# Attention logits of a graph network: four buffers of lifted one-hots, running maxima over five chunk slots, maxima between the small logit steps

## The reference, cut to what matters

```python
h = x @ Wn.T + bn
e = edge_attr @ We.T + be
xj = h[src]
a = leaky_relu(sum((xj + e) * attn, axis=-1), 0.01)     # one logit per edge
m = segment_max(a, dst, num_segments=N)                 # greatest logit of each destination node
a = exp(a - m[dst])
a = a / (segment_sum(a, dst, num_segments=N)[dst] + 1e-16)
out = relu(segment_sum(xj * a[:, None], dst, num_segments=N))
```

## Time and profile before

| | us |
|---|---|
| median of three runs | 4340.02 (4337.76 to 4342.67) |
| the profiled execution, its own time | 4305.89 |
| its span, first to last instruction | 4304.1 |
| stretch of the logit steps, first `expand` of the block loop to the end of the last reduction | 426.7 |

### The profile page before, as it was taken

How to read it: one execution, slowest core, us unless ns; L and a number is a source line. 1 busy time by engine, 2 the same in 40 slices (tenths; PEclk the granted TensorE clock), 3 DMA queues, 4 the chain that set the end, 5 groups by cost and what they waited for, 6 DMA issues and landing times. The chain is left out here.

```text
span 4304.1 us, 87013 instructions
## 1 busy us (share of the span) xinstructions
PE 3335.9 (78%) x18482; PEld 2452.3 (57%) x18483; DVE 2751.1 (64%) x9374; ACT 1717.5 (40%) x5555; POOL 1143.8 (27%) x908
## 2 busy tenths in 40 slices
PE   5555556888888885999943335899998699998988
PEld 4333335777777774676732224777887344544455
DVE  7999999999898884325478886777665300000453
ACT  1555552234344552102178875777774100000111
POOL 1788888888888000101000000000000000000002
PEclk9999999999999997999955557999999899999998
DMA  2444442556677774666666553433331253543046
GB/s 101 116 109 114 111 111 71 141 166 210 197 214 237 275 282 158 182 198 186 196 189 189 181 166 114 152 122 121 106 108 40 93 194 119 182 154 84 3 173 252
DMA packets 437987, 658.37 MB, mean 153 GB/s; under 512 B 98732, under 2 KB 294167, under 8 KB 437762
## 3 DMA queue, kind: packets, MB, share of 16 engines
q1 hardware_dynamic: 354306, 526.63, 38.9%
q10 hardware_dynamic: 53040, 121.95, 7.8%
q0 software_dynamic: 30544, 8.56, 2.8%
HBM read 440.04 MB, written 216.02 MB: 152 GB/s over the span
## 5 line engine op out<-in xcount | busy, mean ns | idle before, releaser
L1007 POOL DMA_INDIRECT slots<-all_B,put_index x800 | 1051.6, 1315 | 342.9 <-issue 237.8
L1889 POOL MEMSET c_T<- 128x28 f32 x1 | 0.1, 148 | 1983.3 <-POOLq L138 1983.3
L770 DVE TENSOR_SCALAR put_hot<-all_iota_bf,put_words_in 128x125 bf16<-128x125 bf16 x2400 | 443.7, 318 | 3.3 <-DMA put_words_in<-slots 3.3
L2437 DVE TENSOR_TENSOR upd_pre<-upd_po,upd_bias 125x512 f32<-125x512 f32 x25 | 17.3, 692 | 621.5 <-PE upd_po L2368 621.5
L1253 ACT ACTIVATE lm_raised<-lm_hot,srt_words 128x125 f32<-128x125 bf16 x1200 | 356.3, 385 | 83.4 <-DVE lm_top L1168 67.8
L981 PE MATMUL put_ps<-put_right_in,put_left_in 128*128 128x125 f32 x2380 | 340.3, 293 | 51.1 <-ACT put_left_in L840 49.1
L1288 PE MATMUL lm_ps<-lm_v,lm_node 125*128 x1220 | 170.2, 184 | 267.2 <-DVEq L1155 95.4
L2012 PE MATMUL att_ps<-att_right,att_left 128*125 128x125 f32 x2380 | 319.5, 286 | 67.2 <-ACT att_right L2033 63.9
L981 PEld LDWEIGHTS put_ps<-put_right_in,put_left_in 128*128 128x128 f32 x2380 | 300.2, 201 | 76.2 <-ACT put_left_in L840 57.9
L2012 PEld LDWEIGHTS att_ps<-att_right,att_left 128*125 128x125 f32 x2380 | 287.0, 190 | 95.7 <-issue 82.2
L840 ACT CAST put_left_in<-put_hot 128x640 f32 (+1 forms) x238 | 173.8, 730 | 415.0 <-DVE put_hot L770 398.3
(11 more groups left out here) (393 smaller groups left out, 5797.6 us busy)
## 6 DMA issues: line engine op xcount, KB each, us to landing
c_T<-counts SPq DMA_DIRECT2D x255, 312.5 KB, 3.3
pair<-put_T ACTq DMA_DIRECT2D x125, 625.0 KB
hot<-put_hot SPq DMA_DIRECT2D x480, 160.0 KB
att_ring<-hot SPq DMA_DIRECT2D x240, 320.0 KB
gio_T<-pair SPq DMA_DIRECT2D x60, 1250.0 KB, 5.9
all_A<-in_edge_attr_dram SPq DMA_DIRECT2D x100, 448.0 KB
lm_planes<-src_rows SPq DMA_DIRECT2D x123, 320.0 KB, 3.7
counts<-put_T ACTq DMA_DIRECT2D x125, 312.5 KB
```

Of the source, the lines that this page charges most:

```text
L770: ins = v.tensor_scalar(hot[:, h, t, c * S:c * S + P], k["iota_bf"][:, :], words_in[:, j, c, t:t + 1], None, ALU.is_equal)
L1007: nc.gpsimd.indirect_dma_start(slots, bass.IndirectOffsetOnAxis(index[:, C * g + j:C * g + j + 1], 0), stage[:, C * g + j, :], None).then_ ...
```

## The change

`raised` gets four buffers (`RING`) in place of two, each split in two halves `u` of five chunks. The running maximum `top` has five chunk slots (625 numbers) in place of ten, and there are two of it, used in turn by even and odd blocks. The first group of a block takes the maximum of its two halves; every other group takes two maxima of 625 numbers, one for each half. In the step, the first maximum stands between the sum and the addition of the edge part, the second between the leaky relu and the subtraction of the floor. The wait for `lifted` moves ahead of the addition. A new semaphore `halved` orders the two maxima. The wait for `joined` at the top of a block now asks for the reduction of the block before the last one.

```diff
-        raised, top8, tops = s.sb("raised", [L, 2, G * P]), s.sb("top8", [L, G * P]), negated
+        raised, top, tops = s.sb("raised", [L, RING, 2, HALF * P]), s.sb("top", [L, 2, HALF * P]), negated
...
-                def total(chain, g):
+                def totals(chain, g):
                     dve.wait_ge(looked, g + 3)
                     chain(v.tensor_reduce(z[:, :], ps[:, ds((g % PZ) * 512, 3 * G)].rearrange("p (c t) -> p c t", t=3), AX.X, ALU.add))
                     dve.sem_inc(summed, 1)
+
+                def with_edges(chain, g):
                     chain(v.tensor_tensor(z[:, :], z[:, :], logit[:, ds(G * g, G)], ALU.add))
...
-                def greater(g, first):
-                    lift = raised[:, ds(g % 2, 1), :].rearrange("p a n -> p (a n)")
-                    dve.wait_ge(lifted, g + 4)
-                    dve.wait_ge(grouped, g + 2)
-                    if first:
-                        ins = v.tensor_copy(top8[:, :], lift)
-                    else:
-                        ins = v.tensor_tensor(top8[:, :], top8[:, :], lift, ALU.max)
-                    ins.then_inc(grouped, 1)
+                def lift(g, u):
+                    return raised[:, ds(g % RING, 1), u, :].rearrange("p a n -> p (a n)")
...
-                for sem, head in ((summed, PZ), (grouped, 2), (joined, 1), (expanded, 2)):
+                for sem, head in ((summed, PZ), (grouped, RING), (joined, 1), (expanded, 2)):
...
-                def step(g, first):
+                def step(d, g, first):
                     chain = Chain(dve, chain_sem, n + 3 * g)
+                    of_block = top[:, ds(d % 2, 1), :].rearrange("p a n -> p (a n)")
                     expand(g + 3)
                     dve.wait_ge(ready, g + 2)
-                    total(chain, g + 2)
-                    logits(chain, g + 2)
-                    greater(g, first)
+                    totals(chain, g + 2)
+                    dve.wait_ge(lifted, g + 4)
+                    if not first:
+                        dve.wait_ge(grouped, g + RING)
+                        v.tensor_tensor(of_block, of_block, lift(g, 0), ALU.max).then_inc(halved, 1)
+                    with_edges(chain, g + 2)
+                    if first:
+                        v.tensor_tensor(of_block, lift(g, 0), lift(g, 1), ALU.max).then_inc(grouped, 1)
+                        dve.sem_inc(halved, 1)
+                        logits(chain, g + 2)
+                    else:
+                        chain(v.scalar_tensor_tensor(z[:, :], z[:, :], 0.01, z[:, :], ALU.mult, ALU.max))
+                        dve.wait_ge(halved, g + 1)
+                        v.tensor_tensor(of_block, of_block, lift(g, 1), ALU.max).then_inc(grouped, 1)
+                        v.tensor_scalar(logit[:, ds(G * (g + 2), G)], z[:, :], floor[:, :], None, ALU.subtract).then_inc(ready, 1)
...
-                    dve.wait_ge(joined, d + 1)
+                    dve.wait_ge(joined, d)
                     dve.sem_inc(passed, 1)
-                    step(g0, True)
+                    step(d, g0, True)
                     with dve.Fori(g0 + 1, g1) as g:
-                        step(g, False)
-                    dve.wait_ge(grouped, g1 + 2)
+                        step(d, g, False)
+                    dve.wait_ge(grouped, g1 + RING)
                     v.tensor_reduce(tops[:, ds(d, 1), :].rearrange("p a n -> p (a n)"),
-                                    top8[:, :].rearrange("p (c n) -> p n c", n=P), AX.X, ALU.max).then_inc(joined, 1)
+                                    top[:, ds(d % 2, 1), :].rearrange("p a (c n) -> p (a n) c", n=P), AX.X, ALU.max).then_inc(joined, 1)
...
-                            ins = nc.scalar.activation(raised[:, j % 2, c * P:(c + 1) * P], hot[:, j, c * S:c * S + P], ACT.Copy,
+                            ins = nc.scalar.activation(raised[:, j, c // HALF, c % HALF * P:c % HALF * P + P], hot[:, j, c * S:c * S + P], ACT.Copy,
                                                        scale=logit[:, ds(G * g + c, 1)])
```

More of the change, by code:

```diff
@@ L1089, in phase_logits @@
             s.sem(n) for n in ("expanded", "looked", "summed", "ready", "lifted", "grouped"))
-        joined, passed, turned, ended = (s.sem(n) for n in ("joined", "passed", "turned", "ended"))
+        joined, passed, turned, ended, halved = (s.sem(n) for n in ("joined", "passed", "turned", "ended", "halved"))
         PZ = 4
@@ L1192, in _ @@
                 expand(1)
-                total(chain, 0)
+                totals(chain, 0)
                 expand(2)
+                with_edges(chain, 0)
                 logits(chain, 0)
                 dve.wait_ge(ready, 1)
-                total(chain, 1)
+                totals(chain, 1)
+                with_edges(chain, 1)
                 logits(chain, 1)
@@ L1212, in _ @@
                     g0, g1 = group_range(dve, k, d)
-                    dve.wait_ge(joined, d + 1)
+                    dve.wait_ge(joined, d)
                     dve.sem_inc(passed, 1)
-                    step(g0, True)
+                    step(d, g0, True)
                     with dve.Fori(g0 + 1, g1) as g:
-                        step(g, False)
-                    dve.wait_ge(grouped, g1 + 2)
+                        step(d, g, False)
+                    dve.wait_ge(grouped, g1 + RING)
                     v.tensor_reduce(tops[:, ds(d, 1), :].rearrange("p a n -> p (a n)"),
-                                    top8[:, :].rearrange("p (c n) -> p n c", n=P), AX.X, ALU.max).then_inc(joined, 1)
+                                    top[:, ds(d % 2, 1), :].rearrange("p a (c n) -> p (a n) c", n=P), AX.X, ALU.max).then_inc(joined, 1)
                 g0, g1 = group_range(dve, k, NB - 1)
+                dve.wait_ge(ready, g1 + 2)
+                dve.sem_inc(passed, 1)
                 with dve.Fori(g1, turns_of(dve, k) * RING) as g:
```

## The result

The changed kernel takes 4359.05 us (median of seven runs, 4350.38 to 4364.82), the kernel before 4340.02 us (seven runs, 4336.79 to 4344.65). The ratio is 1.0042 with a 95% interval of 1.0031 to 1.0053: slower by 0.42%, 19.0 us between the medians. The forecast was slower by 38 us.

What follows compares the result with a forecast made beforehand. VectorE was taken to lead the logit steps, ScalarE to follow. 25 x 3.07 + 94 x 3.40 + 24 x 2.81 + 1.48 = 465.2 us against 426.7, +38.5, gave 4378 us; range 4346 to 4394.

Steps and rivals of the forecast that it cites:

- The two signs named for being wrong: On VectorE: gaps behind sum and leaky relu staying below 0.3 and 0.05 us, or `expand` under 2 us after the reduction.
- Bound: In the logit steps: VectorE leads and ScalarE follows as buffers come free, so four buffers alone bring 0 us.
- Two maxima of 625: VectorE's inner step: each half occupies 0.73 us, the two 1.46, which adds 0.08 us per step.
- The first maximum behind the sum: VectorE's inner step: sum to first maximum takes 0.72 us with two run-time addresses priced; bounds 0.55 and 0.75.
- The second maximum behind the leaky relu: VectorE's inner step: leaky relu to second maximum takes 0.385 us, with bare count and address work; bounds 0.21 and 0.43.
- The loop's work behind 0.88 us of cover: Inner step's end: branch and `expand` addresses, about 0.8 us, stay just covered; floor step to `expand` 0.15 us.
- The step: VectorE's inner step, `expand` to `expand`: 3.40 us against 2.944, so +0.46 us, 94 times.
- First step: First step of each block on VectorE: 3.07 us, 25 times; bounds 2.90 and 3.20.
- The block's end: VectorE, last maximum to next `expand`: 1.06 us to the reduction, then 2.63 whatever its length; +2.81 us, 24 times.
- Rival 1: Inner step: only the extra instruction shows, addresses and counts being cheap; no change at 4340 us, or +3 us; chance 0.15.
- The middle case: Inner steps of 3.12 to 3.3 us, making the kernel 12 to 29 us slower; chance 0.15.
- Rival 2: Block's end: loop bounds load during earlier work, reduction to `expand` 1.22 us; -35 us, 4305 with cheap steps; chance 0.07.

## Why the prediction was right in its direction and wrong in its size

The sign and the range held, and so did the mechanism: sequencer work that no instruction covers. The forecast of +38 us was twice the +19 measured, because one term of the inner step was too large: the addresses ahead of the first maximum. The two signs named for being wrong stayed away, since the gaps are 0.39 and 0.24 us and `expand` follows the reduction after 2.61. Point by point:

- **Bound.** Right: VectorE led and ScalarE followed. Four buffers alone left the stretch at 426.2.
- **Two maxima of 625.** Right: 811 ns each, 0.73 from start to start.
- **The first maximum behind the sum: the term that failed.** Predicted 0.72 us from sum to maximum, measured 0.57 (median). I priced two dynamic addresses (0.25 us and 0.03 for a second piece), by analogy with `expand`. The one of `top` depends on the block alone and was made once per block; the inner step made one, of 117 ns, and with a fixed address of `top` the gap is the same 0.57. 94 times 0.15 is 14 us of the 18 by which the stretch was forecast too long (465.2 against 446.8). The lower bound, one address at 0.55, was the nearer one.
- **The second maximum behind the leaky relu.** Predicted 0.385, measured 0.41.
- **The loop's work behind 0.88 us of cover.** Right in the inner step: floor step to `expand` 0.13 us.
- **The step.** 3.23 us against 3.40 predicted. Of the +0.29 over the step before, 0.12 is the added hole behind the sum, 0.20 the new one behind the leaky relu, 0.08 the second maximum's fixed cost; 0.10 comes back where the maximum no longer waits behind the floor step.
- **First step.** Predicted 3.07, measured 3.09. This is +0.79 us, 25 times, 19.7 us: as much as the whole loss.
- **The block's end.** Reduction to `expand` predicted 2.63, measured 2.61, and shown by the kernel with one slot copied not to hang on the reduction's length. Last maximum to reduction predicted 1.06, measured 0.96: the 0.1 us that I counted for the address of `top` did not show; 25 times 0.1 is another 2.5 us.
- **Rival 1, no change,** had the cheap single address right but not the gap behind the leaky relu. The middle case, which I gave 0.15, had steps of 3.12 to 3.3 and +12 to +29 us; that is what happened. **Rival 2, an end at the engine's pace,** is excluded by the copied slot.
- **A semaphore for nothing.** The rule that a semaphore costs nothing extra and the number of instructions should be lowered (the Trainium skill, VectorE: DVE Perf Modes, "The DRAIN you can't avoid" and "Rules for kernel authors") is borne out here only in part. The added instruction costs its 0.08 us per inner step, 7 us. The sequencer's work in bare places makes the larger part, and one increment that stands alone, moved under cover, was worth 411.2 - 401.8 = 9.4 us.
- **A slip without effect.** The margin of ScalarE's lift is given as 0.4 us; by its own numbers (3.7 less 3.0) it is 0.7. In the changed kernel no maximum waited for ScalarE.

With the measured terms the sum closes: 25 x 3.09 + 94 x 3.23 + 24 x (0.96 + 2.61 - 0.86) + (0.96 + 1.28 - 0.86) = 77.3 + 303.6 + 65.0 + 1.4 = 447.3 us, against 446.8.

## What to carry to other kernels

Before interleaving work to hide a wait, look at which of the sequencer's work (stand-alone waits and increments, address arithmetic, branches, loads of bounds) lies in which gap, and whether an instruction already handed to the engine covers it. A long instruction is worth most ahead of the longest piece of sequencer work: taken from ahead of the loop's entry, one maximum of 0.81 us made the first step 0.62 us longer with the same instructions (3.09 against 2.47). Price addresses by what they depend on: one that depends on an outer loop's variable alone need not be counted in the inner one. And take a change of several parts apart: here the alternating buffers alone gain 15.5 us of stretch (411.2). The halves of five slots behind the floor step lose 33.1 of it again (444.3), and setting them between the small steps another 2.5 (446.8). What the five slots were to give, a reduction of 1.28 us in place of 2.48, is hidden behind the sequencer's 2.6 us at every block's end but the last.

## What was not expected of the hardware

- An increment of a semaphore by VectorE's sequencer cost 0.10 us per step where no instruction covered it, and 0 where 1.38 us of maximum did; behind a 0.23 us instruction it cost 0.11.
- Two executions of one unchanged stage ended 33 us apart, while the stretch of the logit steps agreed with its terms to 0.5 us, and differed by 0.5 and 0.1 us in the two pairs of kernels that differ in the number of buffers alone. Effects under 0.5% of this kernel are read more surely from the stretch than from its whole time, though each stretch is from one execution.
- ScalarE's activations start 0.29 us apart, so ten need 2.90, yet VectorE's inner step ran at 2.84 us, even through the block of 18 groups: ScalarE falls back by about 0.05 us per step, and makes up the lag at each block's end. 22 of the 25 blocks have three to five groups.
